# Two layers behind the neighbour sums of a graph network kernel: eight steps over two rounds instead of two blocks in every second round

## The chip, the cores and the metric

The kernel runs on one core of one Trainium2 chip. The metric is the device time of one execution in microseconds (us), smaller is better.

## What is computed

The reference is a two-stage graph network on 3125 nodes with 256 features and 100,000 edges sorted by target. Only the first stage's graph part matters here:

```python
xn = _layernorm(x, axis=-1)
neigh = jax.ops.segment_sum(node_feats[src], dst, num_segments=n)   # node_feats is xn
h = (1.0 + eps) * node_feats + neigh
h = jax.nn.relu(h @ W1 + b1) @ W2 + b2      # W1 256 x 512, W2 512 x 256
mean = jnp.mean(h, axis=0)
var = jnp.mean(jnp.square(h - mean), axis=0)
h = (h - mean) * jax.lax.rsqrt(var + BN_EPS) * gamma + beta
```

A linear attention, two mixture-of-experts layers and a graph convolution with the same edges follow; the change leaves them alone.

## The kernel before

The program is written engine by engine. Each engine has its own function with its own order of work, and semaphores join them. The stage of the change, the edge stage, turns the edge list into dense 128-column slices of the 3200 x 3200 adjacency matrix and multiplies the features by them. `count_pe`, `count_act` and `count_dve` write out its order by hand for TensorE, ScalarE and VectorE.

**Rounds and steps.** The outer loop runs over rounds `b`, the inner one over eight steps `i`. Rounds 0 to 24 build one slice of 128 target nodes each. The work of later stages of the pipeline lags behind: in round `b` the neighbour sums of slice `b-1` are made, the sums of slice `b-2` are transposed and added, and in every odd round from 3 on the two layers of one pair `q = (b-3)//2` of slices (256 nodes) are done.

- *Hot tiles.* For batch `n = 8*b + i` (two octets of eight target nodes each) `hots_dve` (L993) makes the one-hot tiles with three VectorE operations: L1001, L1002 and, behind a wait, L1006. `hots_pe` (L1011) multiplies them: per octet 12 bf16 matmuls (L1027, L1029) and a last small one (L1032), into one of four banks. The tiles have two buffers, by the parity of the batch, so `hots_dve` of batch `n` waits until TensorE has done batch `n-2` (`win`). TensorE takes two batches back to back at each even step; they are called a burst here. `hots_act` (L1035) copies each octet's bank out (L1048) twice.
- *Sums.* `sums_pe` (L1077) at every step: three or four of 25 row blocks, two fp32r matmuls each (L1088), high and low part of the features. `sums_act` (L1093) copies them at step 0, `turn_sums_pe` (L1099) transposes at step 1, `sums_dve` (L1105, the operation at L1113) adds them into `XT` at step 3.
- *The two layers.* `layer1_pe` (L1119) is eight fp32 matmuls of 256 columns, each two instructions in the trace, into banks 6 and 7: four output chunks `hc`, two input chunks each. `layer1_act` (L1145) adds the bias and applies ReLU into `hidden` (L1150). `layer2_pe` (L1135) is eight more into bank 6 (L1141), and `layer2_act` (L1153) writes the result over `XT` (L1158). `stats_dve` (L1160) takes the batch norm statistics (L1164).

In the order of before, `layer1_pe` stands in one piece behind the sums of step 5 of an odd round and `layer2_pe` in one piece behind those of step 7. `layer1_act` stands at step 6 of that round, `layer2_act` at step 1 and `stats_dve` at step 5 of the even round behind it. Even rounds have no layer work on TensorE. The 13th pair is half as wide (128 nodes) and is done in round 27, when no hot tiles and sums are left. Behind the stage come the batch norm (L1232 to L1242, L1326) and the next stage (`norm_pe`). The SyncE queue stores each finished slice of the adjacency matrix (L1057) and reads `X` back (L1067) once the last is stored.

Of the kernel before, what the change touches and what calls it, by code (L numbers as in the profile page):

```python
# [16 lines left out]
T = 25  # L17
# [23 lines left out]
W_LATE = 16 * 8  # L41
# [30 lines left out]
def program(nc, ctx, a, out):  # L72
    at, sems = {}, {}

    def S(name):
        if name not in sems:
            sems[name] = ctx.enter_context(nc.semaphore(name))
        return sems[name]

    def sb(name, shape, dt=F32):  # L80
        at[name] = nc.sbuf_base
        return ctx.enter_context(nc.sbuf_tensor(name, shape, dt))
# [16 lines left out]
    XT = sb("XT", [128, 2, NP])  # L99
# [20 lines left out]
    w1 = wa[:, 0:1024].rearrange("p (c n) -> p c n", c=2)  # L120
    w2 = wa[:, 1024:2048].rearrange("p (c n) -> p c n", c=4)
# [26 lines left out]
    B = [b[:, :] for b in bankt]  # L148
# [203 lines left out]
    FILLS = 4  # L352
# [67 lines left out]
    def dve_step(f, k):  # L420
        return FILLS + 4 * (f // 2) + 2 * k + f % 2 + 1
# [547 lines left out]
    PAIRED = (T + 1) // 2  # L969
    NB = (OCTETS + 1) // 2  # L970
    hidden = wb_[:, 1024:2048].rearrange("p (h n) -> p h n", h=4)
# [105 lines left out]
    def sums_pe(e, b, i):  # L1077
        bk = B[4 + b % 2]
        if i == 0:
            e.wait_ge(S("cev"), octets_to(b))  # L1080
            if b == 0:
                e.wait_ge(S("xmix"), PAIRS)
                e.wait_ge(S("xnl"), 5)
            if b >= 2:
                e.wait_ge(S("gadd"), b - 1)
        for h in range(T * i // 8, T * (i + 1) // 8):
            for x in (xnh, xnl):
                m = e.matmul(bk[:, 0:D], CNT[b % 2][:, h, :], x[:, h * D:(h + 1) * D],  # L1088
                             start=(h == 0 and x is xnh), stop=(h == T - 1 and x is xnl), skip_group_check=True)
        if i == 7:  # L1090
            m.then_inc(S("gmm"), 1)
# [7 lines left out]
    def turn_sums_pe(e, b):  # L1099
        e.wait_ge(S("sev"), b + 1)  # L1100
        for c in range(2):
            m = e.transpose(B[4 + b % 2][:, D + c * 128:D + (c + 1) * 128], sums[b % 2][:, c * 128:(c + 1) * 128], ident)
        m.then_inc(S("sT"), 1)
# [12 lines left out]
    def pair_cols(q):  # L1116
        return slice(256 * q, min(256 * q + 256, NP))

    def layer1_pe(e, q):  # L1119
        o = pair_cols(q)  # L1120
        w = o.stop - o.start
        e.wait_ge(S("gadd"), min(2 * q + 2, T))
        if q:
            e.wait_ge(S("lay"), 6 * q)
        else:
            e.wait_ge(S("w_late"), W_LATE)
            e.wait_ge(S("key16"), dve_step(FILLS - 1, 0))
        for hc in range(4):
            for c in range(2):
                m = e.matmul(B[6 + hc // 2][:, hc % 2 * 256:hc % 2 * 256 + w], w1[:, c, hc * 128:(hc + 1) * 128], XT[:, c, o],  # L1130
                             start=(hc % 2 == 0 and c == 0), stop=(c == 1), skip_group_check=True)
            if hc % 2:
                m.then_inc(S("layT"), 1)

    def layer2_pe(e, q):  # L1135
        o = pair_cols(q)
        w = o.stop - o.start
        e.wait_ge(S("lay"), 6 * q + 4)
        for c in range(2):
            for hc in range(4):  # L1140
                m = e.matmul(B[6][:, c * 256:c * 256 + w], w2[:, hc, c * 128:(c + 1) * 128], hidden[:, hc, 0:w],  # L1141
                             start=(c == 0 and hc == 0), stop=(hc == 3), skip_group_check=True)
        m.then_inc(S("layT"), 1)

    def layer1_act(e, q):  # L1145
        w = pair_cols(q).stop - pair_cols(q).start
        for hc in range(4):
            if hc % 2 == 0:
                e.wait_ge(S("layT"), 3 * q + 1 + hc // 2)
            e.activation(hidden[:, hc, 0:w], B[6 + hc // 2][:, hc % 2 * 256:hc % 2 * 256 + w], ACT.Relu,  # L1150
                         bias=b1c[:, hc:hc + 1]).then_inc(S("lay"), 1)

    def layer2_act(e, q):  # L1153
        o = pair_cols(q)
        w = o.stop - o.start
        e.wait_ge(S("layT"), 3 * q + 3)
        for c in range(2):
            e.activation(XT[:, c, o], B[6][:, c * 256:c * 256 + w], ACT.Identity, bias=b2c[:, c:c + 1]).then_inc(S("lay"), 1)  # L1158

    def stats_dve(e, q):  # L1160
        o = pair_cols(q)
        e.wait_ge(S("lay"), 6 * q + 6)
        for c in range(2):
            e.bn_stats(bst[:, c, q, :], XT[:, c, o.start:min(N, o.stop)]).then_inc(S("bst"), 1)  # L1164

    def has_batch(b, i):
        return b < T and 8 * b + i < NB

    def layers_at(b):

        return (b - 3) // 2 if b >= 3 and b % 2 else None

    def count_pe(e):
        for b in range(T + 3):
            for i in range(8):
                for j in (i, i + 1) if i % 2 == 0 else ():
                    if has_batch(b, j):
                        hots_pe(e, 8 * b + j)
                if i == 1 and 2 <= b < T + 2:
                    turn_sums_pe(e, b - 2)  # L1180
                if 1 <= b <= T:
                    sums_pe(e, b - 1, i)
                if i == 5 and layers_at(b) is not None:
                    layer1_pe(e, layers_at(b))
                if i == 7 and layers_at(b) is not None:
                    layer2_pe(e, layers_at(b))

    def count_act(e):
        highs_act(e, 2)
        for b in range(T + 4):  # L1190
            for i in range(8):
                if has_batch(b, i):
                    hots_act(e, 8 * b + i)
                if b == 0 and 1 <= i < 6:
                    if i == 1:
                        e.wait_ge(S("fold"), 2 * WG)
                    e.copy(xnh[:, fifth(i - 1)], xn_all[:, fifth(i - 1)]).then_inc(S("xnh"), 1)
                if (b, i) == (0, 6):
                    highs_act(e, 3)
                if b == 1 and i in (2, 4):  # L1200
                    mids_act(e, 1 + i // 2)
                if (b, i) in ((1, 6), (2, 0)):
                    lows_act(e, b + 1)
                if i == 0 and 2 <= b < T + 2:
                    sums_act(e, b - 2)
                if i == 1 and b and layers_at(b - 1) is not None:
                    layer2_act(e, layers_at(b - 1))
                if i == 6 and layers_at(b) is not None:
                    layer1_act(e, layers_at(b))

    def count_dve(e, d):
        e.tensor_scalar(scalec, epsc, goodc, 1.0, ALU.mult, ALU.add).then_inc(S("xts"), 1)
        for b in range(T + 5):
            for i in range(8):
                if has_batch(b, i) and (b or i):
                    hots_dve(e, 8 * b + i)
                if b == 0 and 3 <= i:
                    if i == 3:
                        e.wait_ge(S("xd_out"), 80)
                    e.wait_ge(S("xnh"), i - 2)  # L1220
                    e.tensor_tensor(xnl[:, fifth(i - 3)], xn_all[:, fifth(i - 3)], xnh[:, fifth(i - 3)].bitcast(F32), ALU.subtract).then_inc(S("xnl"), 1)
                if b == 1 and i in (1, 3):
                    first_rest_dve(e, 2 + i // 2)
                if b == 1 and i in (5, 7):
                    second_rest_dve(e, i // 2)
                if i == 3 and 2 <= b < T + 2:
                    sums_dve(e, b - 2)
                if i == 5 and b and layers_at(b - 1) is not None:
                    stats_dve(e, layers_at(b - 1))
        e.wait_ge(S("bst"), 2 * PAIRED)  # L1230
        for c in range(2):
            d.add(e.bn_aggr(bmv[:, c, :], bst[:, c, :, :]))  # L1232
            d.wait()
            e.tensor_scalar(bsc[:, c, 0:1], bmv[:, c, 1:2], 1.0, 1e-5, ALU.mult, ALU.add).then_inc(S("bvar"), 1)
            e.wait_ge(S("bstd"), c + 1)
            d.add(e.reciprocal(bsc[:, c, 0:1], bsc[:, c, 0:1]))
            d.wait()
            d.add(e.tensor_tensor(bsc[:, c, 0:1], bsc[:, c, 0:1], gac[:, c:c + 1], ALU.mult))
            d.wait()
            d.add(e.tensor_tensor(bsc[:, c, 1:2], bmv[:, c, 0:1], bsc[:, c, 0:1], ALU.mult))  # L1240
            d.wait()
            e.tensor_tensor(bsc[:, c, 2:3], bec[:, c:c + 1], bsc[:, c, 1:2], ALU.subtract).then_inc(S("bscale"), 1)  # L1242
# [1396 lines left out]
```

## Time and profile before

| what | us |
|---|---|
| median of 3 runs | 2266.91 (2265.09 to 2268.65) |
| the profiled execution, its own time | 2265.84 |
| its span, first to last instruction | 2264.3 |
| start of round 3, of round 24 in it | 204.62, 573.31 |

All row times count from the start of the span. In a timeline a row is an instruction, or several merged ones (x16), with its start and its length; in brackets stands the idle time of the engine before it, and what ended it. Matmuls overlap in the records: an fp32r matmul of 256 columns is shown with 0.28 us though the next one starts 0.12 us after it. Time lost on TensorE is therefore read from start to start. "issue" as a releaser means that the profile shows nothing that the engine waited for.

### The profile page before, as it was taken

The page shows a single profiled execution, that of the slowest core. Times are in us where ns is not written, and L with a number is a line of the kernel's source. Part 1 is how long each engine was busy: PE and PEld are TensorE (multiplying, and loading weights), DVE is VectorE, ACT ScalarE, POOL GpSimd, SP SyncE. Part 2 cuts the span into 40 slices and gives each one's busy share as a digit, 9 for nine tenths or more (in the row PEclk, how much of TensorE's full clock was granted, in tenths as well). Part 3 has the DMA queues.
Part 4 walks back from the last instruction along what each step waited for, and adds up shares of the span by engine and source line. Part 5 has one row for each costly group of instructions (what it writes and reads, how often), then busy time and mean ns, then how long its engine had stood idle before and what let it go on. Part 6 is the DMA issues. An engine that isn't in the chain of part 4 may idle for free. (4 is left out here: it accounts for less than half of the span.)

```text
span 2264.3 us, 47270 instructions
## 1 busy us (share of the span) xinstructions
PE 2094.6 (93%) x18287; PEld 1966.4 (87%) x18287; DVE 1653.3 (73%) x3119; ACT 1233.8 (54%) x2875; POOL 569.9 (25%) x406
## 2 busy tenths in 40 slices
PE   5559999999879999998999999999999999999996
PEld 3348999999769999997778999899988999999996
DVE  6888877778388888885657655556657867888885
ACT  5565555555437676675533444444435336677674
POOL 3000000000016777773000000000000014777775
PEclk9789999999989999999999999999999999999998
DMA  3413333333547778776001666366651025777776
GB/s 122 142 59 105 102 89 89 112 95 89 160 157 217 222 225 240 222 225 169 20 25 50 184 194 188 98 196 188 188 156 63 20 92 173 226 225 237 232 220 170
DMA packets 241114, 339.04 MB, mean 150 GB/s; under 512 B 33407, under 2 KB 202546, under 8 KB 240754
## 3 DMA queue, kind: packets, MB, share of 16 engines
q1 hardware_dynamic: 208908, 296.19, 41.6%
q0 software_dynamic: 28528, 35.76, 8.5%
q10 hardware_dynamic: 3446, 3.97, 0.5%
q8 instruction: 150, 2.46, 0.5%
q14 instruction: 82, 0.67, 0.1%
HBM read 258.89 MB, written 76.95 MB: 148 GB/s over the span
## 5 line engine op out<-in xcount | busy, mean ns | idle before, releaser
L1977 POOL DMA_INDIRECT SC<-xd,slot_i x128 | 186.5, 1457 | 1461.3 <-DVE slot_q L1613 1332.4
L2371 PE MATMUL bank<-WB_r,XN_r 128*128 128x448 f32 x1400 | 399.7, 367 | 3.7 <-DVE WB_r L2330 3.7
L2330 DVE TENSOR_TENSOR WB_r<-WB,WB_r 128x448 fp32r<-128x448 f32 x350 | 214.0, 624 | 166.1 <-ACT WB_r L2323 166.1
L2323 ACT CAST WB_r<-WB 128x448 fp32r<-128x448 f32 x350 | 197.6, 568 | 222.2 <-PE bank L2371 219.1
L2371 PEld LDWEIGHTS bank<-WB_r,XN_r 128*128 128x128 f32 x1400 | 263.2, 188 | 26.8 <-DVE wb__r L2296 4.4
L1907 PE MATMUL bank<-SC_r,WB_r 128*128 128x256 f32 (+1 forms) x2064 | 250.7, 280 | 8.2 <-issue 7.4
L1907 PEld LDWEIGHTS bank<-SC_r,WB_r 128*128 128x128 f32 x2064 | 244.0, 188 | 12.7 <-issue 12.7
L1048 ACT CAST WB_r<-bank 128x200 fp32r<-128x200 f32 x391 | 140.5, 359 | 194.7 <-PE bank L1032 193.4
L1922 PE MATMUL bank<-R_r,H_r 128*128 128x256 f32 x1752 | 215.1, 282 | 4.8 <-DVE R_r L1818 4.8
L1922 PEld LDWEIGHTS bank<-R_r,H_r 128*128 128x128 f32 x1752 | 208.9, 189 | 5.1 <-issue 5.1
L1770 ACT ACTIVATE wb_<-bank,WB 128x256 f32<-128x256 f32 (+1 forms) x344 | 133.2, 476 | 80.0 <-PE bank L1907 41.3
L1983 POOL DMA_INDIRECT slot_p<-pd,slot_q x128 | 158.7, 1240 | 63.5 <-issue 35.0
L1907 PE MATMUL bank<-SC_r,XN_r 128*128 128x256 f32 x1392 | 170.2, 281 | 3.5 <-issue 2.4
L1907 PEld LDWEIGHTS bank<-SC_r,XN_r 128*128 128x128 f32 x1392 | 165.4, 188 | 7.2 <-issue 6.8
L1779 ACT ACTIVATE yo<-yo,slot_p 128x256 f32<-128x256 f32 x118 | 53.7, 502 | 206.7 <-DVE yo L1857 147.0
L2371 PE MATMUL bank<-WB_r,R_r 128*128 128x448 f32 x448 | 165.1, 369 | 0.0
L1088 PE MATMUL bank<-H_r,WB_r 128*128 128x256 f32 x625 | 164.1, 298 | 0.0
L1088 PE MATMUL bank<-XN_r,WB_r 128*128 128x256 f32 x625 | 153.7, 281 | 0.0
L1048 ACT COPY X<-bank 128x200 f32<-128x200 f32 x391 | 144.6, 370 | 0.0
L1002 DVE TENSOR_TENSOR SC<-R,DR 128x1024 bf16<-128x1024 bf16 x196 | 133.9, 683 | 0.0
L1088 PEld LDWEIGHTS bank<-XN_r,WB_r 128*128 128x128 f32 x625 | 119.1, 190 | 0.0
L1088 PEld LDWEIGHTS bank<-H_r,WB_r 128*128 128x128 f32 x625 | 118.6, 190 | 0.0
(463 smaller groups left out, 5130.4 us busy)
## 6 DMA issues: line engine op xcount, KB each, us to landing
WB<-adjw SPq DMA_DIRECT2D x350, 224.0 KB, 2.9
WB<-in_f_pack SPq DMA_DIRECT2D x127, 512.0 KB
WB<-in_f_pack SPq DMA_DIRECT2D x62, 640.0 KB
adjw<-X SPq DMA_DIRECT2D x24, 1600.0 KB, 7.5
WB<-in_f_pack SPq DMA_DIRECT2D x65, 516.0 KB
xd<-XN SPq DMA_DIRECT2D x15, 640.0 KB, 5.5
y<-X SPq DMA_DIRECT2D x10, 640.0 KB, 3.3
X<-y SPq DMA_DIRECT2D x6, 640.0 KB, 6.5
```

Of the source, the lines that this page charges most:

```text
L1002: e.tensor_tensor(by_two(hot_lo[s][:, 0:m, :]), row(iota16, o), along(lo2, o, 128), ALU.is_equal).then_inc(S("lo1"), 1)
L1048: e.copy(to[b % 2][:, :, 8 * j:8 * j + 8].rearrange("p h (q r) -> p q h r", r=2), bank[:, :, i]).then_inc(S(name), 1)
L1088: m = e.matmul(bk[:, 0:D], CNT[b % 2][:, h, :], x[:, h * D:(h + 1) * D], start=(h == 0 and x is xnh), stop=(h == T - 1 and x is xnl), skip ...
L1770: m = e.activation(st[:, q * w:(q + 1) * w], B[hp][:, q * TS:q * TS + w], gfun[L], bias=b[:, hc:hc + 1])
L1779: e.activation(ob[:, q, :], ob[:, q, :], ACT.Copy, scale=slot_p[:, 2 * i + q:2 * i + q + 1]).then_inc(S("obs"), 1)
L1907: m = e.matmul(B[hp][:, q * TS:q * TS + w], p[:, c * HID + hc * 128:c * HID + (hc + 1) * 128], x[:, c * w:(c + 1) * w], start=(c == 0 and ...
L1922: m = e.matmul(bk[:, s * D:(s + 1) * D], x[:, hc * w + s * 128:hc * w + (s + 1) * 128], p[:, hc * D:(hc + 1) * D], start=(hc == 0 and n == ...
L1977: e.indirect_dma_start(yin[i % 2][:, q * D:(q + 1) * D], None, XD, bass.IndirectOffsetOnAxis(ap=slot_i[:, 2 * i + q:2 * i + q + 1], axis=0 ...
L1983: e.indirect_dma_start(slot_p[:, 2 * i + q:2 * i + q + 1], None, PD.rearrange("(r k) -> r k", k=1), bass.IndirectOffsetOnAxis(ap=slot_q[:, ...
L2323: e.copy(split_w(m)[0], RAW[m % PR]).then_inc(S("whigh"), 1)
L2330: e.tensor_tensor(al, RAW[m % PR], ah.bitcast(F32), ALU.subtract).then_inc(S("wlow"), 1)
L2371: mm_ = e.matmul(conv_bank(k, band, c)[:, 0:PW], x[st][:, o], y, start=(st == 0 and i == 0), stop=(st == T - 1 and i == 2))
```

## The change

`layer1_pe` and `layer2_pe` are cut by `hc` into four parts each, of two matmuls (four instructions of the trace). `PARTS_AT` gives each part a step, counted from the pair's odd round `b`: the first layer at steps 3, 5 and 7 of round `b` and step 0 of round `b+1`, the second at steps 3, 5 and 7 of round `b+1` and step 0 of round `b+2`. `layer1_act` is cut in two halves, one at step 6 of round `b` and one at step 1 of round `b+1`. `layer2_act` and `stats_dve` move from the even round `b+1` to the odd round `b+2`, to steps 1 and 6. The arithmetic, the buffers and the banks are the same.

```diff
--- before.py
+++ after.py
@@ -1116,37 +1116,36 @@
     def pair_cols(q):
         return slice(256 * q, min(256 * q + 256, NP))
 
-    def layer1_pe(e, q):
+    def layer1_pe(e, q, hc):
         o = pair_cols(q)
         w = o.stop - o.start
-        e.wait_ge(S("gadd"), min(2 * q + 2, T))
-        if q:
-            e.wait_ge(S("lay"), 6 * q)
-        else:
-            e.wait_ge(S("w_late"), W_LATE)
-            e.wait_ge(S("key16"), dve_step(FILLS - 1, 0))
-        for hc in range(4):
-            for c in range(2):
-                m = e.matmul(B[6 + hc // 2][:, hc % 2 * 256:hc % 2 * 256 + w], w1[:, c, hc * 128:(hc + 1) * 128], XT[:, c, o],
-                             start=(hc % 2 == 0 and c == 0), stop=(c == 1), skip_group_check=True)
-            if hc % 2:
-                m.then_inc(S("layT"), 1)
-
-    def layer2_pe(e, q):
+        if hc == 0:
+            e.wait_ge(S("gadd"), min(2 * q + 2, T))
+            if q:
+                e.wait_ge(S("lay"), 6 * q)
+            else:
+                e.wait_ge(S("w_late"), W_LATE)
+                e.wait_ge(S("key16"), dve_step(FILLS - 1, 0))
+        for c in range(2):
+            m = e.matmul(B[6 + hc // 2][:, hc % 2 * 256:hc % 2 * 256 + w], w1[:, c, hc * 128:(hc + 1) * 128], XT[:, c, o],
+                         start=(hc % 2 == 0 and c == 0), stop=(c == 1), skip_group_check=True)
+        if hc % 2:
+            m.then_inc(S("layT"), 1)
+
+    def layer2_pe(e, q, hc):
         o = pair_cols(q)
         w = o.stop - o.start
-        e.wait_ge(S("lay"), 6 * q + 4)
+        e.wait_ge(S("lay"), 6 * q + (2 if hc < 2 else 4))
         for c in range(2):
-            for hc in range(4):
-                m = e.matmul(B[6][:, c * 256:c * 256 + w], w2[:, hc, c * 128:(c + 1) * 128], hidden[:, hc, 0:w],
-                             start=(c == 0 and hc == 0), stop=(hc == 3), skip_group_check=True)
-        m.then_inc(S("layT"), 1)
-
-    def layer1_act(e, q):
+            m = e.matmul(B[6][:, c * 256:c * 256 + w], w2[:, hc, c * 128:(c + 1) * 128], hidden[:, hc, 0:w],
+                         start=(c == 0 and hc == 0), stop=(hc == 3), skip_group_check=True)
+        if hc == 3:
+            m.then_inc(S("layT"), 1)
+
+    def layer1_act(e, q, half):
         w = pair_cols(q).stop - pair_cols(q).start
-        for hc in range(4):
-            if hc % 2 == 0:
-                e.wait_ge(S("layT"), 3 * q + 1 + hc // 2)
+        e.wait_ge(S("layT"), 3 * q + 1 + half)
+        for hc in (2 * half, 2 * half + 1):
             e.activation(hidden[:, hc, 0:w], B[6 + hc // 2][:, hc % 2 * 256:hc % 2 * 256 + w], ACT.Relu,
                          bias=b1c[:, hc:hc + 1]).then_inc(S("lay"), 1)
 
@@ -1168,10 +1167,17 @@
 
     def layers_at(b):
 
-        return (b - 3) // 2 if b >= 3 and b % 2 else None
+        return (b - 3) // 2 if b % 2 and 3 <= b < 2 * PAIRED + 3 else None
+
+    PARTS_AT = ((0, 3), (0, 5), (0, 7), (1, 0), (1, 3), (1, 5), (1, 7), (2, 0))
+
+    def layers_pe(e, b, i):
+        for part, (later, at) in enumerate(PARTS_AT):
+            if at == i and layers_at(b - later) is not None:
+                (layer1_pe if part < 4 else layer2_pe)(e, layers_at(b - later), part % 4)
 
     def count_pe(e):
-        for b in range(T + 3):
+        for b in range(T + 5):
             for i in range(8):
                 for j in (i, i + 1) if i % 2 == 0 else ():
                     if has_batch(b, j):
@@ -1180,14 +1186,11 @@
                     turn_sums_pe(e, b - 2)
                 if 1 <= b <= T:
                     sums_pe(e, b - 1, i)
-                if i == 5 and layers_at(b) is not None:
-                    layer1_pe(e, layers_at(b))
-                if i == 7 and layers_at(b) is not None:
-                    layer2_pe(e, layers_at(b))
+                layers_pe(e, b, i)
 
     def count_act(e):
         highs_act(e, 2)
-        for b in range(T + 4):
+        for b in range(T + 6):
             for i in range(8):
                 if has_batch(b, i):
                     hots_act(e, 8 * b + i)
@@ -1203,14 +1206,16 @@
                     lows_act(e, b + 1)
                 if i == 0 and 2 <= b < T + 2:
                     sums_act(e, b - 2)
-                if i == 1 and b and layers_at(b - 1) is not None:
-                    layer2_act(e, layers_at(b - 1))
+                if i == 1 and layers_at(b - 2) is not None:
+                    layer2_act(e, layers_at(b - 2))
                 if i == 6 and layers_at(b) is not None:
-                    layer1_act(e, layers_at(b))
+                    layer1_act(e, layers_at(b), 0)
+                if i == 1 and layers_at(b - 1) is not None:
+                    layer1_act(e, layers_at(b - 1), 1)
 
     def count_dve(e, d):
         e.tensor_scalar(scalec, epsc, goodc, 1.0, ALU.mult, ALU.add).then_inc(S("xts"), 1)
-        for b in range(T + 5):
+        for b in range(T + 6):
             for i in range(8):
                 if has_batch(b, i) and (b or i):
                     hots_dve(e, 8 * b + i)
@@ -1225,8 +1230,8 @@
                     second_rest_dve(e, i // 2)
                 if i == 3 and 2 <= b < T + 2:
                     sums_dve(e, b - 2)
-                if i == 5 and b and layers_at(b - 1) is not None:
-                    stats_dve(e, layers_at(b - 1))
+                if i == 6 and layers_at(b - 2) is not None:
+                    stats_dve(e, layers_at(b - 2))
         e.wait_ge(S("bst"), 2 * PAIRED)
         for c in range(2):
             d.add(e.bn_aggr(bmv[:, c, :], bst[:, c, :, :]))
```

## Rows read from the trace of the kernel before

**Rows 1.** The page, busy time by engine over the span.

```profile
PE 2094.6 (93%) x18287; PEld 1966.4 (87%) x18287; DVE 1653.3 (73%) x3119; ACT 1233.8 (54%) x2875; POOL 569.9 (25%) x406
```

**Rows 2.** Busy time by stretch (length, engines, PEclk, DMA share, GB/s): rounds 6 and 7.

```profile
259.98:274.25 14.27, 13.59 (x262) 13.25 (x260) 13.26 (x27) 9.07 (x35) 0.00 (x0) 1.00 0.28 79
274.25:294.79 20.54, 20.33 (x295) 19.12 (x294) 13.63 (x26) 9.66 (x37) 0.00 (x0) 1.00 0.39 109
```

**Rows 3.** Who waited for whom in rounds 3 to 23: total us, times, longest.

```profile
PE bank L1027 <- issue: 9.2, 31, 0.5
...
DVE wb_ L1001 <- PE bank L1032: 83.2, 32, 3.8
```

**Rows 4.** Timeline of TensorE in round 6, at the middle of three bursts.

```profile
264.19 0.17 PE L1032 MATMUL bank<-R 128*128 128x8 bf16 x1
264.33 0.20 PE L1027 MATMUL bank<-SC 128*128 128x100 bf16 x1
...
267.07 0.17 PE L1032 MATMUL bank<-R 128*128 128x8 bf16 x1
267.10 0.20 PE L1027 MATMUL bank<-wb_,SC 128*128 128x100 bf16 x1
...
267.49 0.17 PE L1032 MATMUL bank<-R 128*128 128x8 bf16 x1
...
267.87 0.20 PE L1027 MATMUL bank<-SC 128*128 128x100 bf16 x1 [0.21 <-issue]
...
271.03 0.17 PE L1032 MATMUL bank<-R 128*128 128x8 bf16 x1
271.66 0.20 PE L1027 MATMUL bank<-SC 128*128 128x100 bf16 x1 [0.47 <-issue]
```

**Rows 5.** Timeline of VectorE in round 6, from the statistics to batch 7.

```profile
267.68 0.75 DVE L1164 BATCH_NORM_STATS2 small<-XT 128x6 f32<-128x256 f32 x2
...
268.34 0.35 DVE L1001 TENSOR_TENSOR wb_<-R,DR 128x400 bf16<-128x400 bf16 x1
...
269.91 0.36 DVE L1001 TENSOR_TENSOR SC<-R,DR 128x400 bf16<-128x400 bf16 x1
```

**Rows 6.** Timeline of TensorE: sums, then a layer block, in rounds 7 and 25.

```profile
282.97 0.37 PE L1088 MATMUL bank<-H_r,WB_r 128*128 128x256 f32 x1
283.17 0.28 PE L1088 MATMUL bank<-XN_r,WB_r 128*128 128x256 f32 x1
283.29 0.28 PE L1088 MATMUL bank<-H_r,WB_r 128*128 128x256 f32 x1
...
284.48 3.61 PE L1130 MATMUL bank<-XT,wa 128*128 128x256 f32 x16
...
287.93 0.21 PE L1027 MATMUL bank<-wb_,SC 128*128 128x100 bf16 x1
...
587.11 3.61 PE L1130 MATMUL bank<-XT,wa 128*128 128x256 f32 x16
...
590.68 0.28 PE L1088 MATMUL bank<-XN_r,WB_r 128*128 128x256 f32 x1
```

**Rows 7.** Timeline of ScalarE in round 7, the four ReLUs of a pair.

```profile
289.40 1.60 ACT L1150 ACTIVATE wb_<-bank,cols 128x256 f32<-128x256 f32 x4
```

**Rows 8.** Timeline of the stage's end: the last, half-wide pair.

```profile
595.68 0.38 PE L1102 MATMUL bank<-CB,yo 128*128 128x128 f32 x2
...
596.86 2.02 PE L1130 MATMUL bank<-XT,wa 128*128 128x128 f32 x16 [0.80 <-ACT XT L1158]
598.03 0.62 ACT L1150 ACTIVATE wb_<-bank,cols 128x128 f32<-128x128 f32 x2 [1.31 <-PE bank L1130]
...
599.60 2.05 PE L1141 MATMUL bank<-wb_,wa 128*128 128x128 f32 x16 [0.71 <-ACT wb_ L1150]
```

**Rows 9.** Timeline of SyncE's queue: `X` read back behind the last store.

```profile
583.98 4.10 SPq L1067 DMA_DIRECT2D X<-y  x5
```

**Rows 10.** Weight loads of the first layer by line in rounds 1 to 27 (busy, mean ns).

```profile
L1130 PEld LDWEIGHTS bank<-XT,wa 128*128 128x128 f32 x208 | 37.4, 190 | 5.4 <-DVE XT L1113 1.0
```

## The prediction

> **What bounds the kernel now.** I read the busy times first, then the stretches of the edge stage, then the waits, and then a timeline of one round. TensorE is busy for 93% of the span [rows 1], so it is the engine to look at, but that share is an average. In the edge stage an even round (no layers) takes 14.27 us and an odd one (both layers) 20.54 us, 34.81 together, at full clock. What to see there is VectorE: 13.26 us busy in the short round, 13.63 in the long one [rows 2]. It has the same work in both, 93% of the one and 66% of the other. So VectorE is nearly level with TensorE in even rounds and has 7 us to spare in odd ones. The waits show both sides. TensorE stood idle 31 times before the first matmul of an octet (9.2 us), and VectorE waited 83.2 us for TensorE to free a tile buffer [rows 3]. An engine that is on average idle holds up the busy one, because its slack lies in the wrong round.
>
> The timeline gives the size and the place. Without a wait, the first matmul of an octet starts 0.03 us after the last one of the octet before (267.07 to 267.10). In the middle of the burst of steps 2 and 3, where its second batch begins, the distance is 0.14 (264.19 to 264.33), in that of steps 4 and 5 it is 0.38 (267.49 to 267.87), and in that of steps 6 and 7 it is 0.63 (271.03 to 271.66) [rows 4]. About 0.025 of each is normal, so **0.12, 0.35 and 0.61 us** are lost, 1.08 in this even round. In odd rounds the first two recur and the third does not, since the first layer's block stands before that burst: 0.47. The count fits the waits row: 21 rounds with the middle loss (shown as 0.21 idle) and 10 with the last (0.47) are 31 times and 9.1 us against 9.2. The loss of 0.12 is below what the idle column shows.
>
> **The change part by part.** *Matmuls.* None is added or removed. A layer block of 16 instructions lasts 3.45 us (284.48 to 287.93) [rows 6], so one of the new parts is 0.86. Even rounds gain four parts, odd ones lose four, and 34.81 stays the sum before any stall is counted. Splitting adds boundaries: a pair had two blocks and has eight parts, 78 more over 13 pairs. Between sums and a block, and between a block and a burst, the rows show nothing extra. For the one new kind, a part between two sums (step 0), round 25 has an example: from the block's start to the second sum behind it 3.57 (587.11 to 590.68), which is 3.45 plus one ordinary 0.12 [rows 6]. I take the boundary at zero. The bounds: below, zero, since work cannot shrink; above, 0.08, which is what the first sum behind a burst takes more than the next one (282.97, 283.17, 283.29: 0.20 against 0.12), so up to 6.6 us in all.
>
> *Losses that go.* After the change each burst has one part between it and the burst before it: step 7 before steps 0 and 1, step 0 before 2 and 3, step 3 before 4 and 5, step 5 before 6 and 7. TensorE then reaches the second batch of each burst 0.86 us later after the burst before, while VectorE's work from the freeing of the buffer is the same. All three losses are smaller than 0.86. From round 4 to 23 that is 10 even rounds at 1.08 (10.8) and 10 odd ones at 0.47 (4.7), and in round 3 0.35, as its first part stands at step 3. **Sum 15.85 us**; 15.9 with roundings.
>
> *The statistics, moved.* They are 0.66 us of VectorE (267.68 to 268.34) [rows 5], and go from step 5 of an even round to step 6 of an odd one, so that batch 7 is queued behind them. Queue arithmetic, from the last matmul of batch 4, which frees the buffer of batch 6: in the trace VectorE goes on 0.19 later (267.49 to 267.68), makes batch 6 in 1.57 (268.34 to 269.91), and the first operation of batch 7 lies 1.75 before TensorE can start on it (269.91 to 271.66) [rows 4, 5]. With the statistics between them that is 0.19 + 1.57 + 0.66 + 1.75 = 4.17. TensorE needs it at: 4.17 as in the trace (267.49 to 271.66), less the losses 0.35 and 0.61, plus a part 0.86, 4.07. So 0.10 comes back in each of ten odd rounds: **-1.0 us**. Batches 4 and 5 have the addition of sums (L1113) before them as now, but a loss of 0.35 against a part of 0.86.
>
> *ScalarE.* It is busy 9.07 us in the short round [rows 2], and the four ReLUs of a pair take 1.60 [rows 7]; half of them come in each of two rounds. In step 1 the half waits for the part at step 0, and the copies of batch 2 queue behind it. That part ends before TensorE starts batch 2, whose first octet is done over a microsecond later, and the pair of ReLUs takes 0.8. Its cover is thus the sums of step 1 and an octet; without it a late copy would hold a bank and cost at most that 0.8. I take zero. *New waits of the parts.* The second layer's first part waits for ReLUs five steps old, its third for ReLUs made at step 1 while it stands at step 7. The first part of a pair (step 3 instead of 5) waits for L1113, which VectorE issues right after batch 3; TensorE still has batch 3 (two octets of 0.42, as from 267.07 to 267.49 [rows 4]) and 12 sums of 0.12 before it, 2.3 us. Zero. On SyncE no DMA moves; `X` is read back 15 us before the stage ends [rows 9] and shifts with the stores.
>
> *The stage's end.* Two parts of pair 11's first layer and all its second fall behind the last sums. That is the same TensorE work, and the first half of the second layer covers the ReLUs. But the transposes (595.68) [rows 8] stood in the wait for L1158 and now come earlier: +0.2. For the last pair the second layer's first half need not wait for all four ReLUs: the first two end at 598.65, so it starts near 598.7 and is done when the block now starts (599.60) [rows 8]. Half of 2.05, so -0.9. Together 0.7 us gained. Bounds 0 and 1.
>
> **The sum**: 15.85 - 1.0 + 0.7 = 15.5 us. Against the profiled execution 2265.84 - 15.5 = 2250.3; that execution lies 1.07 below the median, so against the median 2251.4, which I give.
>
> **A rule against it.** The loss repeats with the same size in each round of its kind [rows 3, 4]. The Trainium skill, *Perfetto Trace Analysis*, section Optimization Strategy, says that such a repeating gap on the engine that should be saturated can mean too few buffers for the next tile. The change adds no buffer. By that rule taken alone the sum would be zero and the time 2266.9.
>
> **The rivals.** *The buffers hold it up anyway.* Each batch starts only when the one two before it is multiplied, in either order of the layers. If this chain and not the total of the work set the loss, it would stay: 2266.9. For it: the two-deep chain is there, 83.2 us of waiting for it [rows 3]. Against it: where the first layer's block stands before a burst, in odd rounds, the loss of steps 6 and 7 is gone. 5%.
>
> *Boundaries at the upper bound.* 78 times 0.08 is 6.6 us back: 2258. Against it are rows 6, with one example of the new kind only. 10%.
>
> *Weights exposed, slower.* If each part had to wait for its first weight load on the way in and the sums or the burst for theirs on the way out, 0.19 us each [rows 10], 78 x 0.38 = 29.6 us come back: 2251.4 + 29.6 = 2281. It decides from 0.20 us per added boundary (15.5 / 78); above that the kernel is slower than before. Rows 6 show none of it at 3.45, 3.57. 4%. The Trainium skill, *TensorE: Matmul & The Clock Gate*, section The mechanism, says that a weight load overlaps a running matmul only when the row groups differ, and here all are full height. The rows disagree: sums follow each other at 0.12 us, less than one load.
>
> *Clock or transfers downstream.* The stages behind start 15 us earlier with nothing else changed, but waits and clock steps there may fall otherwise. A few us either way, mostly back: 2256. 6%.
>
> **How the numbers follow.** Forecast 75%, the four rivals 5, 10, 4 and 6%. The runs shown spread by 3.6 us, so 0.2% (4.5 us) is about what can be told from no change. Faster means under 2262.4: 75 + 10 + 6 = 91, less 1 for stragglers, 90%. Same 6%, slower 4%. The forecast's own bounds are 2248 (all of the 15.85, end at 1, half the spread) and 2255; the range goes up to 2259 to take in the second rival, and down to 2247.
>
> **What would show it.** Right: even and odd rounds both near 16.6 us, 33.3 to 33.5 together; the waits row of L1027 down from 9.2 us to under 1, left only at step 7 of odd rounds; TensorE's busy sum about unchanged per instruction. Wrong: parts that last over 0.90 from start to next start, waits on L1130 or L1141 in rounds 3 to 24, ScalarE copies late at step 2, or the loss of steps 4 to 7 still there.

## The result and the profile after

| | before | after |
|---|---|---|
| median of 6 runs, us | 2266.54 (2261.93 to 2268.65) | 2251.05 (2248.73 to 2251.31) |
| ratio, 95% interval | | 0.9932 [0.9919, 0.9945] |
| profiled execution: span | 2264.3 | 2249.4 |
| start of round 3 in it | 204.62 | 197.83 |
| from the start of round 3 to the last matmul of the second layer ("the stage" below) | 396.8 | 380.9 |
| from that last matmul to the end of the span ("behind the stage") | 1662.9 | 1670.7 |

The forecast was 2251.4. The stage is 15.9 us shorter. The two other lines of the table nearly cancel: round 3 starts 6.8 us earlier though nothing ahead of it was changed, and the part behind the stage is 7.8 us longer. The first two experiments are about that.

The page after, span and busy time:

```profile
span 2249.4 us, 47270 instructions
PE 2094.8 (93%) x18287; PEld 1966.0 (87%) x18287; DVE 1659.0 (74%) x3119; ACT 1234.4 (55%) x2875; POOL 566.6 (25%) x406
```

The same instructions and the same busy time of TensorE (2094.8 against 2094.6) [rows 1] in a span that is 15 us shorter: only idle time went. Rounds 6 and 7 after, in the columns of [rows 2]:

```profile
247.02:263.62 16.60, 16.60 (x277) 15.81 (x276) 13.34 (x25) 8.94 (x35) 0.00 (x0) 1.00 0.39 111
263.62:280.36 16.74, 16.74 (x278) 15.89 (x277) 13.99 (x27) 9.65 (x37) 0.00 (x0) 1.00 0.32 91
```

14.27 and 20.54 us have become 16.60 and 16.74, together 33.34 instead of 34.81, and TensorE is shown busy all the time. Who waited for whom in rounds 3 to 23; in TensorE's answer no row stands under the heading, and VectorE's has one:

```profile
engine line waited for: us in total, times, longest us
...
DVE wb_ L1001 <- PE bank L1032: 60.2, 73, 1.2
```

In TensorE's list 31 waits and 9.2 us stood before [rows 3]. VectorE still waits 60.2 us for buffers, but in 73 pieces of at most 1.2 us instead of 32 of up to 3.8. It waits less in all, and no longer in a few long pieces in every second round.

Of the losses one is left. TensorE in round 7, from the middle of burst 4 and 5 to that of burst 6 and 7:

```profile
272.72 0.17 PE L1032 MATMUL bank<-R 128*128 128x8 bf16 x1
272.75 0.20 PE L1027 MATMUL bank<-SC 128*128 128x100 bf16 x1
...
276.75 0.17 PE L1032 MATMUL bank<-R 128*128 128x8 bf16 x1
...
276.92 0.20 PE L1027 MATMUL bank<-SC 128*128 128x100 bf16 x1
```

and VectorE beside it:

```profile
272.93 0.37 DVE L1001 TENSOR_TENSOR wb_<-R,DR 128x400 bf16<-128x400 bf16 x1 [0.80 <-PE bank L1032]
...
274.50 0.75 DVE L1163 BATCH_NORM_STATS2 small<-XT 128x6 f32<-128x256 f32 x2
275.17 0.35 DVE L1001 TENSOR_TENSOR SC<-R,DR 128x400 bf16<-128x400 bf16 x1
```

The middle of burst 4 and 5 passes in 0.03, without a loss. In burst 6 and 7 it is 0.17, so 0.14 is lost. The queue is the predicted one: buffer free at 272.72, batch 6 from 272.93, statistics at 274.50, batch 7 from 275.17, TensorE on it at 276.92: 0.21 + 1.57 + 0.67 + 1.75 = 4.20. But VectorE's first row also shows it idle for 0.80 us ahead of batch 6.

A part, between sums and the transposes, and one between sums and a burst:

```profile
249.36 0.28 PE L1088 MATMUL bank<-XN_r,WB_r 128*128 128x256 f32 x1
249.47 1.02 PE L1130 MATMUL bank<-XT,wa 128*128 128x256 f32 x4
250.34 0.38 PE L1102 MATMUL bank<-CB,yo 128*128 128x128 f32 x2
...
271.06 1.02 PE L1130 MATMUL bank<-XT,wa 128*128 128x256 f32 x4
...
271.92 0.21 PE L1027 MATMUL bank<-wb_,SC 128*128 128x100 bf16 x1
```

0.87 and 0.86 from start to start, against a quarter of a block, 0.86 [rows 6].

### The profile page after: what moved, and what is told of

Read it like the earlier page. It is cut to its first block and busy times, and to the rows that moved or that the text cites. A ratio compares the mean times of both kernels' runs of the same rounds, so it can differ in the third digit from the quotient of the medians.

```text
span 2249.4 us, 47270 instructions
## 1 busy us (share of the span) xinstructions
PE 2094.8 (93%) x18287; PEld 1966.0 (87%) x18287; DVE 1659.0 (74%) x3119; ACT 1234.4 (55%) x2875; POOL 566.6 (25%) x406
```

## The experiments

"Stage" is always from the first matmul of round 3 to the start of the last matmul of the second layer in the profiled execution. The kernel before was timed beside each set on the same chip.

**Both kernels once more.**

> The kernel before once more, unchanged, for a second profile. In the first pair of profiles round 3 starts 6.8 us earlier in the changed kernel though nothing ahead of it differs, and 7.8 us of the gain are gone again behind the edge stage. If both are chance of single executions, this profile shows the edge stage from the start of round 3 to the last layer matmul at 396.9 us within 0.3 again, while the start of round 3 can lie anywhere between about 197 and 205. If the change itself moves the early part, round 3 starts at 204.6 here.

> The changed kernel once more. Chance: the edge stage from round 3 to the last layer matmul takes 381.0 us within 0.3 again, and the start of round 3 need not be at 197.8. Systematic: it is at 197.8 again and the part behind the stage is again 7.8 us longer than in the kernel before.

Measured: the kernel before 2263.2 us, the changed one 2246.8, one run each. In the second profile of the kernel before, its first row of round 3 and the summary of the second layer (first and last start):

```profile
196.05 0.22 PE L1027 MATMUL bank<-wb_,SC 128*128 128x100 bf16 x1
...
L1141 PE MATMUL bank<-wb_,wa x208: 275/379/379, 213.1 to 593.0; 128*128 128x256 f32 x96, 128*128 128x128 f32 x8
```

and in that of the changed kernel:

```profile
197.69 0.22 PE L1027 MATMUL bank<-wb_,SC 128*128 128x100 bf16 x1
...
L1140 PE MATMUL bank<-wb_,wa x208: 275/378/382, 221.0 to 578.6; 128*128 128x256 f32 x96, 128*128 128x128 f32 x8
```

Stages of 396.9 and 380.9, against 396.8 and 380.9 in the first pair. Round 3 now starts at 196.1 in the kernel *before*, so the 6.8 us do not come from the change. The changed kernel starts it at 197.7 once more, as the systematic reading also had it, but a third profile of it, further below, starts at 206.5. Behind the stage the two differ by 2.0 (1668.8 and 1666.8) the other way. Over all profiles of the study round 3 starts between 196 and 206, and what lies behind the stage takes 1663 to 1674; why these parts vary the record does not show. The stage alone repeats to 0.2 us, and it carries the comparison from here on.

**One block in each round.** Level rounds, but not level steps.

```diff
-    PARTS_AT = ((0, 3), (0, 5), (0, 7), (1, 0), (1, 3), (1, 5), (1, 7), (2, 0))
+    PARTS_AT = ((0, 5), (0, 5), (0, 5), (0, 5), (1, 5), (1, 5), (1, 5), (1, 5))
```

> The first layer stays one block at step 5 of the odd round, the second becomes one block at step 5 of the even round. My theory (a loss goes only where layer work stands between two bursts): the even round loses only its 0.61 at steps 6 and 7, and the 0.12 and 0.35 of both rounds stay, while the statistics now fall into the odd round behind its block. Gain about 10 x 0.61 = 6.1 us, 2260.5; stalls left before L1027 in rounds 3 to 23 about 0.47 a round. Rival (the mean load of the rounds counts, and equal rounds are enough): the rounds are as level as in the changed kernel, so nearly the whole gain, 2251 to 2253.

Measured: 2256.85 against 2262.56 before, 0.9976 [0.9963, 0.999], so -5.7; stage 391.0 (-5.8). Rounds 11, 5 and 6, then the waits of TensorE, read here and in the next experiments up to 545 us of the span:

```profile
333.95:351.05 17.10, 16.89 (x279) 16.17 (x277) 13.82 (x28) 9.64 (x37) 0.00 (x0) 1.00 0.34 98
231.27:248.36 17.09, 16.88 (x279) 16.16 (x277) 13.82 (x28) 9.66 (x37) 0.00 (x0) 1.00 0.35 98
248.36:265.45 17.09, 16.88 (x278) 16.17 (x277) 13.16 (x26) 8.92 (x35) 0.00 (x0) 1.00 0.35 98
```

```profile
PE bank L1027 <- issue: 3.8, 18, 0.2
...
```

Odd and even rounds are now alike, at 17.09 to 17.11 us but for three of 17.20 to 17.25, and VectorE is idle 3.3 us in an odd and 3.9 us in an even one. Still 0.47 is lost in nearly every round, most of it (0.35) at steps 4 and 5. Level rounds are not enough; the rival falls.

**Eight parts in four steps.**

```diff
-    PARTS_AT = ((0, 3), (0, 5), (0, 7), (1, 0), (1, 3), (1, 5), (1, 7), (2, 0))
+    PARTS_AT = ((0, 3), (0, 3), (0, 7), (0, 7), (1, 3), (1, 3), (1, 7), (1, 7))
```

> The eight parts are put in twos, at steps 3 and 7 of both rounds. My theory: the 0.35 of steps 4 and 5 goes in 21 rounds (7.4 us), the 0.12 stays, and steps 6 and 7 have no layer work before them in either round. In odd rounds they now hold the statistics too, queued behind batch 6, and lose about 0.9; in even rounds about 0.2. So 11 us come back against 6.1 us that go: total gain near 1 to 3 us, 2264 to 2266. Rival (level rounds are enough): 2251 to 2253.

Measured: 2263.18 against 2262.56, 1.0006 [0.9992, 1.002]: no difference. The stage is 395.8, 1.1 less than before, at the low end of what was expected. Rounds 11 and 12, then the waits:

```profile
335.66:353.38 17.72, 16.87 (x278) 16.08 (x276) 13.80 (x27) 9.67 (x37) 0.00 (x0) 1.00 0.33 94
353.38:370.45 17.07, 16.88 (x278) 16.09 (x277) 13.18 (x25) 8.97 (x35) 0.00 (x0) 1.00 0.35 98
```

```profile
PE bank L1027 <- DVE SC L1002: 7.6, 9, 0.8
PE bank L1027 <- issue: 2.1, 11, 0.2
```

The loss of steps 4 and 5 is gone in both rounds and that of steps 6 and 7 is 0.99 in odd rounds and 0.34 in even ones (expected 0.9 and 0.2). Here the profile names VectorE as the releaser. The same cut of the layers, over the same two rounds, gives next to nothing if it skips the steps that need it.

**One VectorE operation more, in both orders.** The rival here is that the losses have nothing to do with VectorE.

```diff
+    spare = sb("spare", [128, 6, 50], BF16)
...
+        part_of_o = slice(o.start, o.start + min(m, 6))
+        e.tensor_tensor(by_two(spare[:, 0:min(m, 6), :]), row(slot16, part_of_o), along(key2, part_of_o, KEYS), ALU.is_equal).then_inc(S("key1"), 1)
         e.tensor_tensor(key, row(slot16, o), along(key2, o, KEYS), ALU.is_equal).then_inc(S("key1"), 1)
...
-        e.wait_ge(S("key1"), n + 1)
+        e.wait_ge(S("key1"), 2 * n + 2)
```

> The kernel before with one VectorE operation more in each batch (six of the eight windows of L1001 once more, into a spare tile; about 0.22 us). My theory: VectorE's chain of two batches grows by 0.44 us for each burst, TensorE's by nothing, so every loss of even rounds grows by about 0.44 and new ones open in odd rounds before the block: about +28 us in all (some 4 of them in rounds 0 and 1). If the losses had another cause than VectorE's lateness (bank copies, TensorE's own queue), the time moves by the 4 us of the first rounds alone.

> The changed kernel with the same VectorE operation added. My theory: a part of 0.86 us before each burst leaves room for the 0.44, except at steps 6 and 7 of odd rounds, where the loss of 0.14 grows to about 0.5: some 4 to 5 us, and 4 in rounds 0 and 1, so about +9 us. The two orders are then 34 us apart instead of 15. Rival (equal slowing of both, the order does not matter): +28 us as in the kernel before.

Measured, against 2263.17: with the order of before 2292.92, 1.0127 [1.0108, 1.0145], so +29.8 (expected +28); with the new order 2255.31, 0.9962 [0.9948, 0.9976]. Stages 420.4 and 385.8, that is +23.5 and +4.9 (4 to 5 expected for the second); the orders are 34.6 us apart in the stage (expected 34) and 37.6 in the medians. TensorE's waits with the order of before:

```profile
PE bank L1030 <- issue: 19.0, 39, 0.7
PE bank L1030 <- DVE SC L1005: 7.4, 9, 0.8
```

and with the new one:

```profile
PE bank L1030 <- issue: 4.5, 11, 0.4
```

(L1030 is L1027 moved by three lines.) From round 4 on the new order loses 0.58 at step 7 of odd rounds and nothing elsewhere. A VectorE that is 0.22 us slower in each batch costs 23.5 us in one order and 4.9 in the other. This is the cleanest sign that the losses were VectorE's lateness and that a part ahead of each burst covers it: neither the copies out of the banks nor TensorE's own queue was touched.

**Single matmuls at sixteen steps.** The price of a boundary. Each part is cut into its two matmuls, at consecutive steps, and ScalarE's operations move behind them.

```diff
-    PARTS_AT = ((0, 3), (0, 5), (0, 7), (1, 0), (1, 3), (1, 5), (1, 7), (2, 0))
+    PARTS_AT = ((0, 3), (0, 4), (0, 5), (0, 6), (0, 7), (1, 0), (1, 1), (1, 2), (1, 3), (1, 4), (1, 5), (1, 6), (1, 7), (2, 0), (2, 1), (2, 2))
...
-                if i == 1 and layers_at(b - 2) is not None:
+                if i == 3 and layers_at(b - 2) is not None:
                     layer2_act(e, layers_at(b - 2))
-                if i == 6 and layers_at(b) is not None:
+                if i == 7 and layers_at(b) is not None:
                     layer1_act(e, layers_at(b), 0)
-                if i == 1 and layers_at(b - 1) is not None:
+                if i == 3 and layers_at(b - 1) is not None:
                     layer1_act(e, layers_at(b - 1), 1)
```

> Each part is cut again into its two matmuls, which stand at sixteen steps in a row (from step 3 of the odd round to step 2 of the next odd one). 88 more boundaries for whole pairs and 16 for the last. My theory: a boundary costs nothing, so the stage from round 3 on takes 380.5 us within 1. By the upper bound of the prediction (0.08 a boundary) it would be 8 us longer, by a wait for a weight load on both sides (0.38) 40 us.

Measured: 2251.83 (4 runs), 0.9941 [0.9921, 0.9961]; stage 386.3, 5.4 longer than the changed kernel, which my theory did not allow. Rounds 11 and 12, and TensorE's waits:

```profile
329.76:347.02 17.26, 16.95 (x278) 15.86 (x277) 13.99 (x27) 9.84 (x37) 0.00 (x0) 1.00 0.34 98
347.02:363.58 16.56, 16.56 (x277) 15.72 (x276) 13.33 (x25) 8.95 (x35) 0.00 (x0) 1.00 0.36 100
```

```profile
PE bank L1130 <- ACT XT L1157: 3.1, 10, 0.3
```

The even round, with eight single matmuls at its eight steps, is not longer (16.56 against 16.60). The odd one is, and the waits say why: the last matmul of a pair stands at step 2, its copy on ScalarE at step 3, and the next pair's first matmul, at step 3 too, waits for the bank. The experiment had brought in a wait of its own. So it was made again with the last two matmuls together and the copy a step earlier. The edit, against the sixteen:

```diff
-    PARTS_AT = ((0, 3), (0, 4), (0, 5), (0, 6), (0, 7), (1, 0), (1, 1), (1, 2), (1, 3), (1, 4), (1, 5), (1, 6), (1, 7), (2, 0), (2, 1), (2, 2))
+    PARTS_AT = ((0, 3), (0, 4), (0, 5), (0, 6), (0, 7), (1, 0), (1, 1), (1, 2), (1, 3), (1, 4), (1, 5), (1, 6), (1, 7), (2, 0), (2, 1), (2, 1))
...
-                if i == 3 and layers_at(b - 2) is not None:
+                if i == 2 and layers_at(b - 2) is not None:
```

> As the sixteen single matmuls, but the last two stand together at step 1 and the copy behind them at step 2, so that the next pair's first part, at step 3, finds its bank free. The sixteen lost 0.5 us in each odd round. My theory: that was the wait of the next pair for this copy and no price of a boundary, so odd rounds go from 17.25 back to 16.73 and the stage from 386.3 to about 381. If boundaries cost something after all, odd rounds stay above 17.

Measured: 2257.85 (4 runs) on a chip where the kernel before takes 2274.28, 0.9928 [0.9911, 0.9946]; stage 380.3. Rounds 11 and 12:

```profile
336.43:353.14 16.71, 16.71 (x278) 15.80 (x276) 13.98 (x27) 9.72 (x37) 0.00 (x0) 1.00 0.36 102
353.14:369.70 16.56, 16.56 (x277) 15.72 (x276) 13.33 (x25) 8.95 (x35) 0.00 (x0) 1.00 0.36 100
```

16.71 and 16.56 against 16.74 and 16.60 with about half as many boundaries. A boundary costs nothing here, and both rivals that priced it are out.

**The statistics one step earlier.**

```diff
-                if i == 6 and layers_at(b - 2) is not None:
+                if i == 5 and layers_at(b - 2) is not None:
                     stats_dve(e, layers_at(b - 2))
```

> The changed kernel with the statistics at step 5 of the odd round instead of step 6, so ahead of batch 6 and not behind it. VectorE waits there for the buffer of batch 6 anyway, so most of the 0.66 us is hidden: the 0.14 at step 7 of ten odd rounds goes and the stage is 1.4 us shorter (379.1). Rival: the queue to batch 7 is the same length in both orders, as in the sum of the prediction, and nothing changes. On the whole time 1.4 us is near what can be told.

Measured: 2246.84 against 2263.17, 0.9923 [0.9906, 0.9939]; stage 379.5, 1.3 shorter than the changed kernel. Rounds 11 and 12:

```profile
329.61:346.21 16.60, 16.60 (x277) 15.81 (x276) 14.00 (x27) 9.67 (x37) 0.00 (x0) 1.00 0.31 89
346.21:362.81 16.60, 16.60 (x277) 15.81 (x276) 13.34 (x25) 8.96 (x35) 0.00 (x0) 1.00 0.40 114
```

No loss is left from round 4 to round 23. TensorE's last matmul of batch 4 in round 7, and VectorE's statistics and batch 6:

```profile
272.31 0.17 PE L1032 MATMUL bank<-R 128*128 128x8 bf16 x1
```

```profile
271.64 0.74 DVE L1163 BATCH_NORM_STATS2 small<-XT 128x6 f32<-128x256 f32 x2
272.51 0.37 DVE L1001 TENSOR_TENSOR wb_<-R,DR 128x400 bf16<-128x400 bf16 x1
```

VectorE does the statistics in the time in which it waited for batch 6's buffer, and still takes the buffer 0.20 us after it is free (0.21 in the changed kernel). Then both were timed side by side.

> The changed kernel, timed beside the next one on one chip. Stage 380.9 us; 0.6 to 0.7% under the kernel before.

> The statistics at step 5, beside the changed kernel on one chip. The stage is 1.3 us shorter in the trace (379.5 against 380.9); if nothing behind it takes that back, the medians differ by about 1.3 us, at the edge of what can be told.

Measured, with the kernel before at 2274.28: the changed kernel 2260.29, 0.9936 [0.9919, 0.9953]; with the earlier statistics 2258.57, 0.9924 [0.9905, 0.9942]. Stages 380.9 and 379.5 once more. The 1.3 us are plain in the stage in two pairs of profiles. In the whole time the medians differ by 1.7 the same way, but the intervals overlap, so a gain of the whole kernel is likely and not shown.

## Why the prediction was right

- **The bound.** TensorE is held up by a VectorE that is on average idle: shown by the two kernels with one more VectorE operation. The prediction's first reason, that the slack "lies in the wrong round", is too coarse: level rounds alone gave 5.8 of 15.9 us, and even those are the 0.61 of ten even rounds, where the block now stood ahead of the burst of steps 6 and 7 (6.1 expected). What counts is its second reason, which carried the sum: a part ahead of each burst, that is at the right steps.
- **Losses that go, 15.85.** From round 4 on every loss of before is gone. In round 3 the 0.35 went, as forecast.
- **Statistics, -1.0.** Measured 10 x 0.14 = -1.4. The queue took 4.20 instead of 4.17 and TensorE came at 4.06 instead of 4.07. Right in kind, 0.4 short.
- **Boundaries, 0.** Not zero but slightly a gain. Taking losses and parts off, a round of before lasts 13.19 (even) and 13.17 (odd) and one of after 13.15 and 13.15; over 21 rounds about 0.6 us. The bound of "below, zero" was wrong by that much. The trace shows where most of it lies: the first octet of a burst takes 0.40 us behind fp32r sums and 0.39 behind layer matmuls, and in two rounds six bursts stand behind layer matmuls now instead of two (0.4 us in all).
- **The stage's end, +0.7.** The timeline after:

```profile
570.44 3.62 PE L1140 MATMUL bank<-wb_,wa 128*128 128x256 f32 x16
...
575.08 2.02 PE L1130 MATMUL bank<-XT,wa 128*128 128x128 f32 x16 [1.02 <-ACT XT L1157]
576.24 0.63 ACT L1149 ACTIVATE wb_<-bank,cols 128x128 f32<-128x128 f32 x2 [1.31 <-PE bank L1130]
576.94 2.04 PE L1140 MATMUL bank<-wb_,wa 128*128 128x128 f32 x16
```

`X` was read back 17 us before the stage's end [rows 9], where the prediction says 15; no term used it. The wait for L1158 (L1157 here) grew from 0.80 to 1.02, as said (+0.2). The last pair's second layer starts 1.86 us after its first instead of 2.74 [rows 8], and without a wait (-0.9). From round 24 on the stage takes 31.7 us instead of 28.1, with five parts more in it (4.3 us): 0.7 gained.
- **The sum.** 15.85 - 1.4 + 0.6 + 0.7 = 15.8; measured 15.9 in the stage, 15.5 between the medians, forecast 15.5. Two terms of the sum were off by half a microsecond each, with opposite signs, which is luck. So is part of the agreement in the whole time: the interval on the 15.5 us reaches from about 12 to 18, and in the last set, on another chip, the same change gained 14.0.
- **The rivals.** *The buffers hold it up anyway*: no, the waits row is empty with the same two buffers. The rule of the Trainium skill, *Perfetto Trace Analysis*, section Optimization Strategy, that a repeating gap on the saturated engine can mean too few buffers, does not decide this case: the gaps repeated, and an order of work removed them. A third buffer, the other cure, was not tried. *Boundaries* and *weights exposed*: no, by the sixteen and the fifteen steps. *Downstream*: what lies behind the stage varies by 11 us over the profiles whatever the kernel. No part of it was tied to the change, but differences of a few microseconds there could not be seen.

## What to carry to other kernels

Look at each round of a loop for itself: an engine that is idle a third of the time can still stall the busy one where its queue is only two tiles deep. Here the work that the busy engine does alone was best placed ahead of each point at which it would wait for the other, in pieces a little larger than the wait; equal rounds with the work in one piece gained a third of it (5.8 of 15.9 us), and four pieces in the wrong steps 1.1 us. Small work of the late engine did best ahead of a wait of its own, not behind it.

## What was not expected

Cutting an fp32 block into pieces between fp32r and bf16 matmuls cost nothing on TensorE, down to single matmuls at each step (rounds of 16.56 and 16.71 against 16.60 and 16.74), and a round even became 0.02 to 0.04 us shorter. The Trainium skill, *TensorE: Matmul & The Clock Gate*, section The mechanism, states in its list that a weight load overlaps a running matmul only when the row groups differ, but its opening paragraph also lets a load go ahead into the background weight buffer. The trace does not bear out the "only": full-height loads of 0.19 us [rows 10] stayed hidden at the boundaries. Which of the two ways the loads took, no run here shows.

The start of round 3 moved by up to 10 us between profiled executions of kernels that are the same up to there (196.1 and 204.6 for the kernel before itself), and the part behind the stage by 11, while all runs of the kernel before beside one set lie within 12 us. The stage in between repeats to 0.2 us. Here the stage, bound by one engine, was measured far better in the trace than through the whole time.
